# Token weights carried in the gathered rows of a mixture-of-experts kernel, and a new order of gathers and weight loads at its start

## What is computed

```python
# x: (4, 512, 512); one of 4 adapters per batch element, rank 16
base = einsum('bsi,oi->bso', x, W_base)
z = einsum('bsj,brj->bsr', einsum('bsi,ji->bsj', x, Wt), A[idx])
y = base + einsum('bso,po->bsp', einsum('bsr,bor->bso', z, B_w[idx]), Wp) * scaling[idx]
probs = softmax(y @ gate_w.T)                 # 2048 tokens, 16 experts
topk_w, topk_idx = top_k(probs, 2);  topk_w /= topk_w.sum()
g, u = y @ w_gate[e].T, y @ w_up[e].T         # 352 wide, for each expert e
expert_out[e] = (silu(g) * u) @ w_down[e].T
out = x + sum over the 2 chosen e of topk_w[e] * expert_out[e]
```

## Time and profile before

| | |
|---|---|
| three runs, us | 346.44, 347.85, 349.55 (median 347.85) |
| profiled execution, us | 346.6, of which the span is 344.8 |
| PE busy | 335.8 us, 97% of the span |
| DVE busy | 234.7 us, 68% |
| ACT busy | 178.6 us, 52% |
| POOL busy | 126.3 us, 37% |
| chain that ended last | PE 84%, DMA 7%, DVE 2%, waiting for nothing shown 2% |

### The profile page before, as it was taken

One profiled execution on the slowest core, in us unless ns is written; L12 is line 12 of the kernel. 1 busy time (PEld: TensorE's weight loads), 2 busy tenths in 40 slices (PEclk: granted clock), 3 DMA queues, 4 the chain that ended last, 5 costly groups with the idle time before them and its releaser, 6 DMA issues.

```text
span 344.8 us, 7808 instructions
## 1 busy us (share of the span) xinstructions
PE 335.8 (97%) x1875; PEld 296.7 (86%) x1875; DVE 234.7 (68%) x308; ACT 178.6 (52%) x242; POOL 126.3 (37%) x85
## 2 busy tenths in 40 slices
PE   8999999999999999999999999999999999999993
PEld 4777778788899799899999998999999998989981
DVE  0486699988464658584878857788667588779310
ACT  1498712522545463646557554675445575585221
POOL 0000000022354561428373652747445371344223
PEclk9999999999999999999999999999999999999999
DMA  7990963846599699996999999899988969922154
GB/s 285 391 490 35 439 251 88 328 153 214 177 348 364 147 240 305 259 277 198 311 215 286 312 290 276 231 294 338 314 216 233 263 195 285 306 43 33 11 67 58
DMA packets 47928, 82.49 MB, mean 239 GB/s; under 512 B 5552, under 2 KB 22576, under 8 KB 47792
## 3 DMA queue, kind: packets, MB, share of 16 engines
q1 hardware_dynamic: 38912, 62.96, 55.2%
q0 software_dynamic: 8960, 18.89, 25.0%
HBM read 60.59 MB, written 19.92 MB: 234 GB/s over the span
## 4 chain that ended last, share of the span: by engine, by line
PE 84%; DMA 7%; DVE 2%; issue 2%; POOL 1%; ACT 1%; SPq 1%; POOLq 1%; DVEq 0%; ACTq 0%
PE bank L693 38%; PE bank L722 22%; DMA xg<-y_rows,gidx 4%; PE bank L449 4%; PE bank L549 4%; PE bank L553 4%; PE bank L550 4%; PE bank L667 3%; DMA xs<-xg 2%; PE bank L465 1%; PE bank L480 1%; PE bank L576 1%; POOL out L1250 1%; DMA y_rows<-y_st 1%; SPq L428 1%
## 5 line engine op out<-in xcount | busy, mean ns | idle before, releaser
L1250 POOL DMA_INDIRECT out<-ys,sidx x40 | 77.1, 1928 | 120.4 <-DMA out<-ys,sidx 75.1
L1229 POOL DMA_INDIRECT xg<-y_rows,gidx x40 | 48.7, 1218 | 94.9 <-issue 78.9
L355 DVE TENSOR_TENSOR w_lo<-w_raw,w_hi (+2 forms) x32 | 76.2, 2383 | 9.4 <-issue 6.6
L693 PE MATMUL bank<-w_hi,xt_hi 128*128 x320 | 82.0, 333 | 0.2 <-issue 0.2
L693 PE MATMUL bank<-w_hi,xt_lo 128*128 x320 | 79.1, 324 | 0.0
L693 PE MATMUL bank<-w_lo,xt_hi 128*128 x320 | 79.0, 324 | 0.0
L353 ACT ACTIVATE w_hi<-w_raw (+2 forms) x32 | 64.6, 2020 | 7.9 <-DMA w_raw<-wall 4.0
L847 ACT ACTIVATE sg<-bank 128x352 f32<-128x352 f32 x40 | 18.5, 463 | 76.7 <-PE bank L693 76.6
L693 PEld LDWEIGHTS bank<-w_lo,xt_hi 128*128 128x128 f32 x320 | 56.2, 189 | 0.0
L693 PEld LDWEIGHTS bank<-w_hi,xt_lo 128*128 128x128 f32 x320 | 56.1, 189 | 0.0
L693 PEld LDWEIGHTS bank<-w_hi,xt_hi 128*128 128x128 f32 x320 | 54.6, 189 | 1.4 <-issue 0.8
(11 more groups left out here) (181 smaller groups left out, 363.2 us busy)
## 6 DMA issues: line engine op xcount, KB each, us to landing
w_raw<-wall SPq DMA_DIRECT2D x16, 1408.0 KB, 8.2
w_raw<-wall SPq DMA_DIRECT2D x16, 768.0 KB, 9.9
xs<-xg SPq DMA_DIRECT2D x132, 64.0 KB
x_st<-xin SPq DMA_DIRECT2D x8, 512.0 KB, 13.1
y_rows<-y_st SPq DMA_DIRECT2D x16, 256.0 KB, 4.2
head_sb<-head SPq DMA_DIRECT2D x2, 640.0 KB, 5.1
wb_sb<-wb SPq DMA_DIRECT2D x2, 512.0 KB, 8.8
wbt_sb<-wbt SPq DMA_DIRECT2D x2, 512.0 KB, 10.8
```

What stands on the lines that cost most here:

```text
L355: e.tensor_tensor(w_lo[:, bass.ds(dst, n)], raw, hi, ALU.subtract).then_inc(own, 1)
L693: mm = e.matmul(bank[2 + 2 * s + t % 2][:, 0:INTER], a, w[:, bass.ds(at + (k * GU + s * INTER), INTER)], start=k == 0 and i == 0, stop=k = ...
L1229: e.indirect_dma_start(out=xg[t % NXG][:], out_offset=None, in_=y_dram, in_offset=bass.IndirectOffsetOnAxis(ap=gidx[:, t:t + 1], axis=0)). ...
L1250: e.indirect_dma_start(out=out, out_offset=bass.IndirectOffsetOnAxis(ap=sidx[:, t:t + 1], axis=0), in_=ys[t % NYS][:], in_offset=None, bou ...
```

## The change

Rows of `y_rows` are now 528 numbers wide instead of 512: behind a token's y stand its two weights and 14 zeros. VectorE makes them as `w12`, 16 numbers for each token, right behind the token numbers; SP stores them with one DMA ahead of the store of chunk 12, in pieces of 64 bytes (16 numbers) for 2048 tokens. Gather 0 waits for that DMA (`d_row`). A gathered row brings both weights along; a new VectorE step `weigh(t)` picks one by the choice (`is_top`) and writes one column of `wtab`. The table numbers are coded so that `at_a` tells both the place and the choice. So the second call of `slot_tables`, the splits of the weights and the products into `oh_q` are gone.

GpSimd issues gathers 2 to 7 one behind the other (`N_AHEAD` 8). SP issues the second expert's `gu` part behind the store of chunk 15, its `dn` part when gather 2 has landed, and the third expert's weights when gather 5 has landed (`N_LATE` 5). ScalarE and VectorE change their order around tiles 1 to 7.

```diff
-TABS = 5
+TABS, YW, W_PAD = 3, H + 16, 16
-N_EARLY, C_FLOOR, N_AHEAD = 2, 12, 5
-C_SECOND, N_LATE = CH - 1, 3
+N_EARLY, C_FLOOR, N_AHEAD = 2, 12, 8
+C_ROW, N_LATE = 12, 5
...
                 if c == C_FLOOR:
                     e.wait_ge(d_fill, 16)
+                if c == C_ROW:
+                    e.wait_ge(v_w12, 1)
+                    e.dma_start(y_dram.rearrange("(c p) w -> p c w", p=P)[:, :, H:YW], w12[:]).then_inc(d_row, 16)
                 e.wait_ge(a_y, c + 1)
-                e.dma_start(y_dram[c * P:(c + 1) * P, :], y_st[c % NYST][:]).then_inc(d_y[c % NYST], 16)
-                if c == C_SECOND:
-                    e.wait_ge(v_w12, 1)
-                    for part in PARTS:
-                        e.wait_ge(d_w[part], 16)
-                        load_part(e, part, table(e, T_REX, 1, 0, NEXP - 1), 0)
+                e.dma_start(y_dram[c * P:(c + 1) * P, 0:H], y_st[c % NYST][:]).then_inc(d_y[c % NYST], 16)
...
+            for part in PARTS:
+                e.wait_ge(d_w[part], 16)
+                load_part(e, part, table(e, T_REX, 1, 0, NEXP - 1), 0)
+                e.wait_ge(d_g[N_EARLY], 16)
...
-                        if t == 2 and k == KH // 2:
+                        if t in (1, 2) and k == KH // 2:
                             h_turn(t - 1)
...
             gate_up(0)
-            e.wait_ge(v_ohq, 1)
-            e.wait_ge(v_need, 1)
-            slot_tables(bank[7], 2, TABS - 2)
-            words[1] = tile_word(e, 1)
-            h_turn(0)
             gate_up(1)
...
-            split_weights(e, count, 3, ahead, "gu", a_gu)
             silu(1)
             x_evac(2)
+            split_weights(e, count, 3, ahead, "gu", a_gu)
...
+            def weigh(t, done_by):
+                row = xg[t % NXG]
+                e.wait_ge(d_g[t % NXG], 16 * (t // NXG + 1))
+                e.scalar_tensor_tensor(wtab[:, t:t + 1], row[:, H:H + 1], is_top[:, t:t + 1], row[:, H + 1:H + 2],
+                                       ALU.mult, ALU.max).then_inc(done_by, 1)
...
                     if t == 2:
-                        split_weights(e, count, t + 1, word, "gu", v_gu)
+                        y_low(t + 1)
+                        weigh(t + 1, v_wt)
                     if t <= NFULL:
                         h_low(t - 1)
-                    if t + 1 < N_PE:
+                    if t == 2:
+                        split_weights(e, count, t + 1, word, "gu", v_gu)
+                    if 3 <= t < N_PE - 1:
                         y_low(t + 1)
+                        weigh(t + 1, v_wt)
...
+                    if t + 1 < N_PE:
+                        split_weights(e, count, t + 1, word, "dn", v_dn)
                     if N_PE <= t + 2 < NTILE:
                         y_low(t + 2)
                     if N_PE <= t + 3 < NTILE:
                         x_turned(t + 3)
                     if NFULL <= t < NTILE:
                         h_low(t)
-                    if t + 1 < N_PE:
-                        split_weights(e, count, t + 1, word, "dn", v_dn)
...
+                if t == 0:
+                    e.wait_ge(d_row, 16)
                 e.sem_inc(p_turn, 1)
                 gather(t)
             for i in range(NYST):
                 e.wait_ge(d_y[i], 16 * (CH // NYST))
-            gather(2)
-            e.wait_ge(m_ht, 1)
-            gather(3)
-            e.wait_ge(m_xt, 3)
-            gather(4)
+            for t in range(N_EARLY, N_AHEAD):
+                gather(t)
```

More of the change, by code:

```diff
@@ L86 @@
 SKIP = 4096
-C_ID, C_IQ, C_TOK, C_ADP, C_AT, C_BEF, C_TOP, C_RNK, C_SEL, C_SCL, C_GT, C_IDS, CW = (
-    0, P, P + TQ, *(P + TQ + CH + i for i in range(5)),
-    *(P + TQ + CH + 4 + RANK + i for i in (0, P, P + 1, P + 1 + KH * NEXP, P + 1 + KH * NEXP + NBATCH)))
+C_ID, C_IQ, C_TOK, C_ATK, C_ADP, C_AT, C_BEF, C_TOP, C_RNK, C_SEL, C_SCL, C_GT, C_IDS, CW = (
+    0, P, P + TQ, P + TQ + NSEL, *(P + TQ + NSEL + TOPK + i for i in range(5)),
+    *(P + TQ + NSEL + TOPK + 4 + RANK + i for i in (0, P, P + 1, P + 1 + KH * NEXP, P + 1 + KH * NEXP + NBATCH)))
 R_TRI, R_ONE, R_REV, R_THR, R_CUM, R_TH3, R_IM, RW = 0, P, 2 * P, 2 * P + 16, 2 * P + 32, 2 * P + 288, 2 * P + 293, 3 * P + 293
@@ L200, in build @@
         r_c = region(o_c, C_SIZE)
-        late = [r_c(f"xg{i}", [P, H], F32) for i in range(N_EARLY, NXG)]
+        late = [r_c(f"xg{i}", [P, YW], F32) for i in range(N_EARLY, NXG)]
         ys = [r_c(f"ys{i}", [P, H], F32) for i in range(N_EARLY)]
-        xg = [r_c(f"xg{i}", [P, H], F32) for i in range(N_EARLY)] + late
+        xg = [r_c(f"xg{i}", [P, YW], F32) for i in range(N_EARLY)] + late
         ys += [r_c(f"ys{i}", [P, H], F32) for i in range(N_EARLY, NYS)]
@@ L208, in build @@
         wtab = r_c("wtab", [P, TQ], F32)
-        w12 = r_c("w12", [P, NSEL], F32)
-        w_part = [r_c(f"w_part{i}", [P, NSEL], BF16) for i in range(3)]
-        w_rest = [r_c(f"w_rest{i}", [P, NSEL], F32) for i in range(2)]
+        w12 = r_c("w12", [P, CH, W_PAD], F32)
+        is_top = r_c("is_top", [P, TQ], F32)
         w_top = [r_c(f"w_top{i}", [P, CH], F32) for i in range(2)]
         w_sum, w_inv, w_one = [r_c(n, [P, CH], F32) for n in ("w_sum", "w_inv", "w_one")]
-        tok_a, emp_f = [r_c(n, [P, TQ], F32) for n in ("tok_a", "emp_f")]
+        at_a, emp_f = [r_c(n, [P, TQ], F32) for n in ("at_a", "emp_f")]
         gidx = r_c("gidx", [P, TQ], U32)
@@ L233, in build @@
         g_ps = bank[4][:].rearrange("p (k b n) -> p k b n", k=KH, n=NEXP)
-        y_dram = nc.dram_tensor("y_rows", [NTOK, H], F32, kind="Internal").ap()
+        y_dram = nc.dram_tensor("y_rows", [NTOK, YW], F32, kind="Internal").ap()
         d_cst, d_rc = sem("d_cst"), sem("d_rc")
@@ L314, in x_rows, with weighed @@
             return bank[0][:] if t < N_PE else xt[t % 2][:]
+        def weighed(t):
+            return (v_wt, t + 1) if t < N_PE else (v_wx, t - N_PE + 1)
         def load_part(e, part, ex, at):
@@ L623, in x_turn @@
                     for k in range(KH):
-                        rows = xg[t % NXG][:].rearrange("p (r k) -> p k r", k=KH)[:, k]
+                        rows = xg[t % NXG][:, 0:H].rearrange("p (r k) -> p k r", k=KH)[:, k]
                         mm = e.transpose(bank[0][:, k * P:(k + 1) * P], rows, ident)
@@ L1087, in wide @@
                 return v.unsqueeze(2).to_broadcast([P, NSEL, TQ])
-            def weigh(i):
-                e.tensor_tensor(oh_q[:, :, 2 + i], where, wide(w_part[i][:]), ALU.mult).then_inc(v_chain, 1)
-                done[0] += 1
-            where = oh_q[:, :, 4]
+            where = oh_q[:, :, 2]
             iqs = cs[:, C_IQ:C_IQ + TQ].unsqueeze(1).to_broadcast([P, NSEL, TQ])
@@ L1146, in x_turned @@
                 with in_use(e, count, t):
+                    weigh(t, v_wx)
                     e.wait_ge(d_xs[n % NXS], (n // NXS + 1) * 16 * (P // Q))
@@ L1167, in _ @@
             y_low(0)
-            weigh(1)
-            e.wait_ge(v_chain, done[0])
-            e.tensor_tensor(where, where, wide(w_part[2][:]), ALU.mult).then_inc(v_ohq, 1)
+            weigh(0, v_wt)
             split_weights(e, count, 0, None, "dn", v_dn)
@@ L1174, in _ @@
             y_low(1)
+            weigh(1, v_wt)
             product(0)
-            e.wait_ge(m_tb, 2)
-            step(e.tensor_copy(wtab[:], bank[7][:, 2 * TQ:3 * TQ]))
-            step(e.tensor_tensor(wtab[:], wtab[:], bank[7][:, TQ:2 * TQ], ALU.add))
-            e.tensor_tensor(wtab[:], wtab[:], bank[7][:, 0:TQ], ALU.add).then_inc(v_w, 1)
             h_low(0)
@@ L1185, in _ @@
             y_low(2)
+            weigh(2, v_wt)
             split_weights(e, count, 2, word, "dn", v_dn)
```

58 lines of the change are left out of this document (28 added, 30 removed).

## The result

The changed kernel takes 352.5 us (median of 6 executions, 350.88 to 355.41) where the kernel before took 347.5 beside it (346.44 to 349.55): a ratio of 1.0133, 95% interval 1.0083 to 1.0184. It is slower by 1.3%; the forecast was 347.6, and the range ended at 351.5. The profiled execution took 352.3, with a span of 350.4. Medians are of all executions; ratios and their intervals leave out those more than 1.5% above the fastest of the same kernel, and are not ratios of the medians.

What follows compares the result with a forecast made beforehand. TensorE, busy 97% of the span, was taken to bound the kernel. The terms −2.01 + 1.0 + 0.46 + 1.15 − 0.81 gave −0.2 us, so 347.6 us from a median of 347.85, range 344.6 to 351.5.

Steps and rivals of the forecast that it cites:

- Six gathers at once, and the later loads: Around tile 4: gather 7 comes earlier, third expert's load perhaps a little later, `ht_lo` is ready earlier; −0.81 us.
- the stall at `down(4)`: TensorE's 0.81 us wait for `ht_lo` at 118.71 goes unless tile 7's copies land 1.5 us later; −0.81.
- Table matmuls: 32 matmuls holding TensorE from 83.34 to 85.35 are gone, so it reaches `x_turn(2)` earlier; −2.01 us.
- The store: Token-weight store lands 4.3 us behind its issue at 24.8 ns per packet, so gather 0 delays `x_turn(0)`; +1.0 us.
- rival 1: Store is cheap and the gaps close: 345.8 us, or 344.7 if tile 2's turn is hidden too; chance 0.22.
- Wider rows: Each gather brings 2112 bytes per row instead of 2048, hidden behind a full TensorE from tile 2 on; 0.
- Gather 2: With `dn` out of its way it lands at 88.5, so `x_turn(2)` waits 0.8 us instead of 0.34; +0.46.
- Rival 3: Taking `dn` out of the way does nothing: gather 2 still lands at 90.0; +1.5, 349.1 us; chance 0.06.
- The new order: VectorE's product of tile 2 comes behind the 3.09 us split, so TensorE waits at tile 2's turn; +1.15 us.
- Rival 4: Third expert's load waits for gather 5; tile 7's copies land 3 us later, tile 4's stall grows; 349.9 us; chance 0.07.

Runs made afterwards that it cites:

- c_after: Changed kernel with constants in its waits for the y stores and last scatters, nothing else: 351.24 us, ratio 1.0100 to the kernel before.
- e10: c_after once more, as the control of a later group: 349.16 us, ratio 1.0095 to the kernel before.
- e7: Kernel before without its second slot_tables (32 matmuls) and the waits for them, output wrong: 348.32 us, ratio 0.9984.
- e5: Kernel before with rows of 2112 bytes in DRAM and gather buffers, the added 64 bytes read by nobody: 351.11 us, ratio 1.0036.
- e2: Changed kernel with the second expert's dn part issued right behind its gu part, without waiting for gather 2: 350.04 us, ratio 1.0087.
- e8: Changed kernel with gathers paced as before and N_LATE 3: 347.96 us, ratio 1.0047 to the kernel before.
- e12: e8 with VectorE's gu split at tile 2's turn ahead of h_low(1), as in the kernel before: 346.82 us, ratio 0.9949 to that kernel.
- e6: Changed kernel with N_LATE 3, the six gathers at once kept: 352.42 us, ratio 1.0099 to the kernel before.
- e14: e8 with the edits of both e12 and e13: 346.95 us, ratio 0.9940 to the kernel before.
- e15: e6 once more in a later group: 354.31 us, ratio 1.0134 to the kernel before.
- e4: Changed kernel with ScalarE and VectorE in the order of the kernel before: 351.73 us, ratio 1.0085 to that kernel.
- e1: Changed kernel with the gathers put back in their old pace, N_LATE 5 kept: 350.59 us, ratio 1.0114 to the kernel before.
- e13: e8 with VectorE's transposition of tile 7's rows moved from tile 4's turn to behind tile 5's product: 346.21 us, ratio 0.9923 to the kernel before.
- e3: Kernel before with gathers 2 to 7 issued one behind the other, nothing else of the change: 346.84 us, ratio 1.0003.
- e11: e3 once more in a later group: 346.61 us, ratio 1.0003 to the kernel before.
- e17: e3 a third time, in the last group: 346.62 us, ratio 1.0003 to the kernel before.
- e9: Changed kernel with 52 warming matmuls of 80 columns at the start instead of 20 of 256, to move instruction fetches: 349.03 us, ratio 1.0054.
- the first group: c_after, e1, e2 and e3, run on the same chip with the kernel before beside them: 351.24, 350.59, 350.04 and 346.84 us against 346.29.

## Why the prediction was wrong

The forecast was 4.9 us too low. The step that failed is *Six gathers at once, and the later loads*: it let the gathers go out together at no price, had the later loads "perhaps a little later", and took 0.81 off for the stall at `down(4)`. The runs showed in its place, in the profiled execution of the changed kernel, the hold, 3.98 us of idle time and 2.9 of low clock; the stall's 0.81 does go there, but by luck, as TensorE comes 6.26 us late to the turn of tile 4. In the profiles without the hold (c_after, e10) they showed a wait of 1.08 to 1.52 at tile 4's turn for the third expert's weights, and a stall at `down(4)` that stays. That the six gathers are what brings the hold rests on one group (below); what blocks the increments is open. By the prediction's own steps:

- *Table matmuls, −2.01.* Right in the changed kernel: `x_turn(2)` starts at 88.75, where this step and the store's say 87.70 + 1.0. It is not a price that can be carried to other edits. I did not ask what the 2.01 us covered: in the kernel before, e7 gives 0.2 to 0.6, since `gate_up(1)` stands behind the turn of tile 0, which waits for VectorE's `hh`. In the changed kernel that turn lies inside `gate_up(1)`, which does hide that 1.20.
- *The store, +1.0.* It landed 2.98 us behind its issue, not 4.3, and gather 0 took 3.90, not 3.4. `x_turn(0)` is 0.68 later, with 0.43 of idle time. The packet price was too high, as rival 1 had it, and part came back in the gather. Missed: 0.33 of issue behind it, where TensorE reads the word of tile 1.
- *Wider rows, 0.* e5: between −0.04% and +0.76%, no new gap in its profile; neither 0 nor 2 us is excluded.
- *Gather 2, +0.46.* `x_turn(2)` does not wait at all; the gather issued at 83.60 was there by 88.75, so in under 5.15 us instead of 7.95. Rival 3 fell, and e2 is its counterpart: with `dn` ahead, `x_turn(2)` waits 1.48.
- *The new order, +1.15 at the turn of tile 2.* 0.94 in c_after, e10 and e8, with the mechanism as told: product behind the split of 3.09. The right term. That the old order would be better by it was not said and is not so (e12).
- *The stall at `down(4)`, −0.81.* Wrong where TensorE is not held up: 0.66 in c_after, 0.89 in e10. VectorE's row of the transposition, at 115.25 in the earlier trace rows, in e10:

```profile
117.82 1.13 DVE L1147 STREAM_TRANSPOSE xt<-xs 128x512 f32<-128x512 f32 x1 [2.19 <-DMA xs<-xg]
```

  The copies land 2.6 us later, more than the 1.5 that the step allowed for, as SP first issues them at 108.96 (106.29 before), behind the later loads. What is saved on TensorE ahead of such a landing is given back there, as in e7.
- *Rival 4, the loads run late*, had the right sign (ScalarE waits for the third expert's weights, and the copies of tile 7 land 2.6 later), but not the cause, the place or the chance (0.07): SP issues the load only 0.4 later than before (93.6; 93.2), it lands 11.5 us behind its issue instead of 7.0, and the cost, 1.08 to 1.52, stands at tile 4's turn, beside the stall.

By e10 and c_after, where the hold is absent: −2.01 −0.34 −0.23 + 0.68 + 0.33 + 0.94, and 1.1 to 1.5 for the late weights, with the stall about as it was. That is +0.5 to +0.9. The traces agree: the turn of tile 5 starts 0.90 later in e10 and 1.02 in c_after than in the kernel before (120.89). e10's span is 1.6 longer in the end; the other 0.7 arises near 235, where ScalarE waits for a later expert's weights and TensorE behind it:

```profile
232.24 2.56 ACT L357 ACTIVATE w_hi<-w_raw  x1 [1.84 <-DMA w_raw<-wall]
```
```profile
235.76 0.55 PE L673 MATMUL bank<-cs,hh 128*128 128x128 f32 x3 [0.30 <-DVE hh L1162]
```

Waits of this kind are a cost that neither the forecast nor its rivals had. Between 126 and 285 us four of the thirteen profiles of kernels with the change have a wait of TensorE of 1.0 us or more (c_after, e6, e14, e15: near 194 and 242 behind a late split of weights on ScalarE, in e14 also at 144 behind late copies); none of the seven profiles without it has one of 0.1. Why the transfers run late there is open. The medians of e10 and of the kernel before beside it differ by 2.5, and at full clock still by 2.3 (348.94, 346.62), so the low clock in 2 of the 6 executions is a small part. e10's profiled execution is the fastest of its six, and what the others lost no profile shows.

- *The hold.* In no step and no rival. It is 3.98 of idle time and 2.9 of low clock, so it is more than the whole error of the forecast. It was found in four profiles (the changed kernel, e4, e6, e15), all with six gathers at once in a kernel without the second table matmuls, and never in a paced one (e1, e8, e12, e13, e14), nor with the burst in the kernel before (e3, e11, e17; no low clock in 34 executions). In c_after, e2, e9 and e10, kernels of the first kind too, it was absent from the profile. So the burst makes the hold likelier in kernels with the change: e15 against e12, e13 and e14 (a low clock in 6 of 6 and in 4 of 36 executions) shows that in one group. Only one execution of each kernel was profiled, and the first group shows no gain from pacing. That the removed matmuls are needed as well is likely and not shown, as e3, e11 and e17 all ran while the kernel before kept its clock. What blocks TensorE's increments is open. Two things coincide with it: the landings of gathers 4 to 7, and a 16 KB fetch on the queue for instructions, which the DMA records have at 85.4 before and at 88.8 now. That fetch alone does not do it: without the burst e1, e7, e8, e12, e13 and e14 have it at 87.5 to 88.7, and none had the hold; nor do both together always, as c_after (88.6) and e10 (88.0) show. e9 was to separate the two, with the fetch moved to 82.1, and met no hold.

## What to carry to other kernels

Before taking work off the busiest engine, look past it for the next wait that ends at a time of its own, such as a transfer: e7 removed 2.01 us of work and gained 0.2 to 0.6. Do not let transfers out in a burst just because their buffers are free, and price what is queued behind them: in one group the paced kernels took 346 to 347 us where the one with the burst took 354, though the same burst cost the kernel before nothing in three groups. And price a long stall above its length: the five of 3.25 to 4.12 us here cost a further 1.4 to 2.9 us by the half clock behind them.

## What the hardware showed that I had not expected

A store of 2048 pieces of 64 bytes landed in 2.98 us, against 1.99 for 256 KB in large rows. The Trainium skill ("DMA: Bandwidth & Descriptors", Specifications) warns of pieces under 512 bytes; here the penalty is 1 us in all. In the hold a semaphore increment of TensorE reached the other engines 4.8 us after the matmul that carries it is recorded as done, while its next matmuls ran. The same kernel before took 346.3 in one group and 349.2 in another on the same chip; its clock was low in 1 of 19 and in 13 of 29 executions, and at full clock it took 346.3 and 347.3, so this is most of the difference and not all. No profile caught where the clock fell.
